# Self-attention of a perceiver layer: queries and values placed in other ways, and the tile's steps in another order

## What is computed

```
x = x + xattn(layernorm(x), ctx, ctx, mask)          # part 1, 257 context rows
x = x + attn(layernorm(x), Wq, bq, ..., Wo, bo)      # part 2, 32 positions
x = x + ffn(layernorm(x), 8 experts, top 2)          # part 3

def attn(x):                                         # B=128, N=32, D=128, H=16, dk=8
    Q, K, V = (proj(Wq, bq), proj(Wk, bk), proj(Wv, bv))     # (x @ W + b), split in heads
    scores = einsum('bhnd,bhmd->bhnm', Q, K) / sqrt(dk)
    scores = scores + power_law_mask(N, 0.25)        # -0.25 log(i-j); -inf above the diagonal
    out = einsum('bhnm,bhmd->bhnd', softmax(scores), V)
    return out @ Wo + bo
```

## Time and profile before

| | us |
|---|---|
| median of 3 runs (lowest, highest) | 981.73 (981.18, 982.58) |
| the profiled execution: its own time | 979.43 |
| its span in the profile | 977.7 |
| PE / DVE / ACT / POOL busy in the span | 828.2 / 829.6 / 661.4 / 448.4 |

### The profile page before, as it was taken

How to read it: one execution, slowest core, us unless ns; L and a number is a source line. 1 busy time by engine, 2 the same in 40 slices (tenths; PEclk the granted TensorE clock), 3 DMA queues, 4 the chain that set the end, 5 groups by cost and what they waited for, 6 DMA issues and landing times. The chain is left out here.

```text
span 977.7 us, 30213 instructions
## 1 busy us (share of the span) xinstructions
PE 828.2 (85%) x9453; PEld 668.0 (68%) x9453; DVE 829.6 (85%) x2343; ACT 661.4 (68%) x2102; POOL 448.4 (46%) x437
## 2 busy tenths in 40 slices
PE   4989889898889988896788888887989889889892
PEld 2666656666666666664678888887888788788782
DVE  4888889888898988986688887874899999999994
ACT  3677777777677777774676666663777677677674
POOL 3222222222222222221454444443677887787785
PEclk9999999999999999999799998999999999999997
DMA  3221111111111111131000000000000000000000
GB/s 85 75 73 49 48 39 49 36 49 48 36 49 41 46 49 38 49 104 61 1 1 0 0 0 0 0 1 1 1 7 11 5 5 11 5 5 11 5 5 17
DMA packets 32695, 27.26 MB, mean 28 GB/s; under 512 B 3548, under 2 KB 32408, under 8 KB 32664
## 3 DMA queue, kind: packets, MB, share of 16 engines
q1 hardware_dynamic: 32664, 26.87, 9.5%
HBM read 24.76 MB, written 2.10 MB: 27 GB/s over the span
## 5 line engine op out<-in xcount | busy, mean ns | idle before, releaser
L545 ACT ACTIVATE E<-SC,neg_max 128x257 f32<-128x257 f32 x512 | 235.9, 474 | 101.7 <-DVE neg_max L605 101.7
L605 DVE TENSOR_REDUCE neg_max<-SC 128x1 f32<-128x257 f32 x512 | 181.9, 418 | 36.4 <-PE SC L402 33.6
L415 PE MATMUL ETP<-ident,E 128*128 128x128 f32 x1024 | 162.8, 287 | 37.7 <-ACT E L545 37.3
L614 DVE TENSOR_TENSOR Et<-ETP,mask_T 128x512 f32<-128x512 f32 x256 | 172.6, 684 | 15.9 <-PE ETP L415 14.8
L415 PEld LDWEIGHTS ETP<-ident,E 128*128 128x128 f32 x1024 | 109.4, 142 | 88.3 <-issue 78.7
L1337 PE MATMUL PO<-W,hid 128*128 128x128 f32 x1024 | 138.1, 278 | 18.8 <-ACT hid L1378 18.8
L1402 ACT ACTIVATE Y<-Z,zb,zs 128x128 f32<-128x128 f32 x256 | 111.0, 485 | 59.9 <-DVE zb L1557 59.9
L1337 PEld LDWEIGHTS PO<-W,hid 128*128 128x128 f32 x1024 | 131.4, 192 | 29.0 <-issue 21.6
L1326 PE MATMUL PH<-xT,W 128*128 128x256 f32 x512 | 135.1, 387 | 0.5 <-ACT xT L1370 0.5
L1378 ACT ACTIVATE hid<-PH,b1c 128x256 f32<-128x256 f32 x256 | 105.5, 463 | 19.4 <-PE PH L1326 17.8
L545 ACT ACTIVATION_READ_ACCUMULATOR E<-SC,neg_max 128x1 f32 x512 | 103.8, 203 | 0.0
(11 more groups left out here) (163 smaller groups left out, 1551.3 us busy)
## 6 DMA issues: line engine op xcount, KB each, us to landing
V<-in_ctx_dram SPq DMA_DIRECT2D x64, 256.0 KB, 2.7
xh<-in_x_dram SPq DMA_DIRECT2D x32, 64.0 KB, 2.2
last_rep<-in_ctx_dram SPq DMA_DIRECT2D x128, 2.0 KB
X<-in_x_dram SPq DMA_DIRECT2D x32, 64.0 KB
out_dram<-Xo SPq DMA_DIRECT2D x64, 32.0 KB, 1.5
W<-in_L_ffn_w_dram SPq DMA_DIRECT2D x1, 1024.0 KB
W<-in_L_ffn_w_dram SPq DMA_DIRECT2D x2, 512.0 KB
b2r<-in_L_ffn_b_dram SPq DMA_DIRECT2D x1, 512.0 KB
```

The costliest lines, as they stand in the source:

```text
L415: i = pe.transpose(ETP[s][:, c:c + P], E[:, j // HB, NQ * (j % HB) + 2 * s + u, k * P:(k + 1) * P], ident[:, :])
L545: i = act.activation(E[:, h, at, :], SC[:, u, 0:S], ACT.Exp, bias=neg_max[:, j % 2, u:u + 1], accum_out=den[:, h, at:at + 1])
L605: dve.tensor_reduce(neg_max[:, j % 2, u:u + 1], SC[:, u, 0:S], AX.X, ALU.max, negate=True).then_inc(max_sb, 1)
L614: dve.tensor_tensor(Et[:, 2 * (j % 2) + s, :, :, :].rearrange("p u k c -> p (u k c)"), ETP[s][:, :], mask_T[:, :, :, :].rearrange("p u k c ...
```

## The change

- **Queries.** `Qt` and `front` are gone. ACT writes `Qbd` straight from `PA`, 4 instructions of 128x256 (one for each q), with `hh_scaled` as per-partition scale and `bq_own` (a new constant, mask times bias, one small DVE instruction in the setup) as per-partition bias.
- **Values.** `xT4`, `repeated` and `Vbd` are gone. PE computes each 32x32 block by itself: weights are a batch of `xT` (128x32), the moving operand is 32 columns of `Wv`, and the output goes to the 32 partitions of its group in one bank `PV`. That is 32 matmuls a tile in place of 8. ACT copies the whole bank, 128x256, in one instruction to `Vt`, which has two buffers, as `xT` now has.
- **Weighing.** In place of a 128x128 matmul with a block diagonal, four of 32 rows x 32 columns, one for each g, on the diagonal tiles of the array: 32 matmuls a tile in place of 8, each still with 128 moving columns.
- **Order.** PE does `project_out` two tiles late (t-2) and right behind `scores(t, 0)`; before, it stood last in the body, for t-1. DVE has `add(t-2)` behind the second `less_maxima`, and `sums(t, 0)` behind both. Two bodies more, of T and T+1, finish the last tiles.
- **No hardware loop** in `attend`: all tiles are in straight line. The clear of `Vbd` in the setup is gone.

```diff
+                dve.tensor_scalar(bq_own[:, :], hh_scaled[:, :, 0], bcol[:, 0:1], None, ALU.mult).then_inc(dve_set2, 1)
-                pool.memset(Vbd[:, :, :], 0.0).then_inc(pool_set2, 1)
 def run(body, eng):
-            body(0, 2, False)
-            body(1, 2, True)
-            with eng.Fori(2, T - 2) as t:
-                body(t, 2, True)
-            body(T - 2, 1, True)
-            body(T - 1, 0, True)
+            for t in range(T - 2):
+                body(t, True, True, t > 0, t > 1)
+            body(T - 2, True, False, True, True)
+            body(T - 1, False, False, True, True)
+            body(T, False, False, True, True, False)
+            body(T + 1, False, False, False, True, False)
 # DVE body (conditions left out)
                     maxima(t, 1)
-                    sums(t, 0)
                     less_maxima(t, 1)
+                    add(t - 2)
+                    sums(t, 0)
                     invert(t, 0)
                     own(t - 1, 0)
                     own(t - 1, 1)
                     norm(t + 2)
                     sums(t, 1)
                     invert(t, 1)
-                    add(t - 1)
 # POOL body
-                    bias(t - 1)
+                    bias(t - 2)
                     power(t + 2)
-                    front(t + 1)
                     normalise(t, 0)
                     normalise(t, 1)
 # ACT
-                    act.activation(Qt[:, :, :].rearrange("p b l -> p (b l)"), PA[:, 0:256], ACT.Identity,
-                                   bias=bcol[:, 0:1]).then_inc(qt_sb, 1)
+                    for q in range(HQ):
+                        i = act.activation(Qbd[:, :, q, :], PA[:, 0:256].rearrange("p (b l) -> p b l", b=TB), ACT.Identity,
+                                           bias=bq_own[:, q:q + 1], scale=hh_scaled[:, q, 0:1])
+                    i.then_inc(q_bd, 1)
-                    for g in range(NQ):
-                        r = slice(32 * g, 32 * g + 32)
-                        i = act.activation(Vbd[r, HB * h:HB * h + HB, 32 * g:32 * g + 32],
-                                           PV[h][r, :, 32 * g:32 * g + 32], ACT.Copy)
+                    act.activation(Vt[:, t % 2, :, :], PV[:, :, :], ACT.Copy).then_inc(v_sb, 1)
 # PE
-                    for j in range(HB):
-                        i = pe.matmul(PV[h][:, j, :], xT4[:, HB * h + j, :, :].rearrange("p g l -> p (g l)"), W["v"][:, :],
-                                      start=True, stop=True)
+                    for b in range(TB):
+                        for g in range(NQ):
+                            i = pe.matmul(PV[32 * g:32 * g + 32, b, :], xT[:, t % 2, b, :], W["v"][:, 32 * g:32 * g + 32],
+                                          start=True, stop=True)
                     for j in range(HB):
-                        i = pe.matmul(PE_[h][:, j, :], Vbd[:, HB * h + j, :], Et[:, h, j, :], start=True, stop=True)
+                        for g in range(NQ):
+                            r = slice(32 * g, 32 * g + 32)
+                            i = pe.matmul(PE_[h][r, j, :], Vt[r, t % 2, HB * h + j, :], Et[r, h, j, :], start=True, stop=True)
```

More of the change, by code:

```diff
@@ L69, in perceiver_layer @@
         bcol = sb("bcol", [P, 3])
+        bq_own = sb("bq_own", [P, HQ])
         out_bias = sb("out_bias", [P, D])
@@ L721, in _ @@
                 turn_tile(T - 1)
-        attend(nc, X, ident, hh_scaled, (W, hh_wide, decay, out_bias, bcol, neg_half2, Kbd, Vbd))
+        attend(nc, X, ident, hh_scaled, (W, hh_wide, decay, out_bias, bcol, bq_own, neg_half2, Kbd))
         mix_experts(nc, X, ident, (G, W1, W2, b1c, b2r, gr, b_rows, iota_f, neg_half3, w3_in), out)
@@ L738, in sem @@
             return s2.enter_context(nc.semaphore(name))
-        W, hh_wide, decay, out_bias, bcol, neg_half, Kbd, Vbd = consts
+        W, hh_wide, decay, out_bias, bcol, bq_own, neg_half, Kbd = consts
         stat = sb("stat2", [P, 2, 6])
@@ L745, in attend @@
         xn = sb("xn2", [P, 2, D])
-        xT = sb("xT2", [P, TB, L])
-        xT4 = sb("xT4", [P, TB, NQ, L])
-        Qt = sb("Qt2", [P, TB, L])
+        xT = sb("xT2", [P, 2, TB, L])
+        Vt = sb("Vt2", [P, 2, TB, L])
         Qbd = sb("Qbd2", [P, TB, HQ, L])
@@ L758, in attend @@
         PA = ps("PA", [P, 512])
-        PV = [ps(f"PV{h}", [P, HB, D]) for h in range(2)]
+        PV = ps("PV", [P, TB, L])
         PS = [ps(f"PS{h}", [P, 512]) for h in range(2)]
@@ L861, in add, with body @@
                     dve.tensor_tensor(tile_of(t), PY[:, :], Xb[:, :], ALU.add).then_inc(x2, 1)
-                def body(t, after, before):
-                    if after > 1:
+                def body(t, one_more, two_more, one_back, two_back, now=True):
+                    if two_more:
                         norm_stats(t + 2)
-                    add_decay(t, 0)
-                    if after > 1:
+                    if now:
+                        add_decay(t, 0)
+                    if two_more:
                         norm_mean(t + 2)
-                    maxima(t, 0)
-                    if after > 1:
+                    if now:
+                        maxima(t, 0)
+                    if two_more:
                         norm_var(t + 2)
-                    add_decay(t, 1)
-                    less_maxima(t, 0)
-                    maxima(t, 1)
-                    sums(t, 0)
-                    less_maxima(t, 1)
-                    invert(t, 0)
-                    if before:
+                    if now:
+                        add_decay(t, 1)
+                        less_maxima(t, 0)
+                        maxima(t, 1)
+                        less_maxima(t, 1)
+                    if two_back:
+                        add(t - 2)
+                    if now:
+                        sums(t, 0)
+                        invert(t, 0)
+                    if one_back:
                         own(t - 1, 0)
                         own(t - 1, 1)
-                    if after > 1:
+                    if two_more:
                         norm(t + 2)
-                    sums(t, 1)
-                    invert(t, 1)
-                    if before:
-                        add(t - 1)
+                    if now:
+                        sums(t, 1)
+                        invert(t, 1)
                 for t in range(2):
@@ L998, in probs, with body @@
                     act.activation(Et[:, h, :, :], PE_[h][:, :, :], ACT.Copy).then_inc(et_sb, 1)
-                def body(t, after, before):
-                    if after > 0:
+                def body(t, one_more, two_more, one_back, two_back, now=True):
+                    if one_more:
                         turned(t + 1)
-                    if before:
+                    if one_back:
                         probs(t - 1, 0)
                         probs(t - 1, 1)
-                    exponentials(t, 0)
-                    if after > 0:
+                    if now:
+                        exponentials(t, 0)
+                    if one_more:
                         projected(t + 1)
[L1009 to L1013, removed]
+                    if now:
+                        exponentials(t, 1)
+                        values(t)
                 turned(0)
                 projected(0)
-                repeated(0)
                 run(body, act)
-                probs(T - 1, 0)
-                probs(T - 1, 1)
             @block.tensor
@@ L1088, in project_out, with body @@
                     i.then_inc(y_ps, 1)
-                def body(t, after, before):
-                    if after > 0:
+                def body(t, one_more, two_more, one_back, two_back, now=True):
+                    if one_more:
                         turn(t + 1)
-                    scores(t, 0)
-                    if before:
+                    if now:
+                        scores(t, 0)
+                    if two_back:
+                        project_out(t - 2)
+                    if one_back:
                         turn_probs(t - 1, 0)
-                    scores(t, 1)
-                    if before:
+                    if now:
+                        scores(t, 1)
+                    if one_back:
                         turn_probs(t - 1, 1)
-                    if after > 0:
+                    if one_more:
                         project(t + 1)
-                    values(t, 0)
-                    if before:
+                    if now:
+                        values(t)
+                    if one_back:
                         weigh(t - 1, 0)
                         weigh(t - 1, 1)
-                    values(t, 1)
-                    if before:
-                        project_out(t - 1)
                 turn(0)
```

73 lines of the change are left out of this document (23 added, 50 removed).

## The result

| | before | after |
|---|---|---|
| median of 4 runs each (lowest, highest), us | 982.15 (981.18, 983.01) | 950.89 (949.44, 952.09) |
| ratio, with its 95% interval | | 0.9681 [0.9665, 0.9698] |
| the profiled execution: its own time, its span | 979.43, 977.7 | 950.97, 949.1 |
| `attend`: first DVE instruction to first score addition | 10.9 | 12.1 |
| first score addition of tile 0 to that of tile 15 | 181.5 | 150.4 |

The kernel became 31 us faster, 28.6 of it in the spans of the two profiled executions. All of it lies between the first additions of tiles 0 and 15: 31.1 less, and 3.0 more at the two ends of `attend`. `attend` itself begins 0.4 earlier. The medians differ by 2.7 more than the spans, because before's profiled execution (979.43) lies 2.7 under its median of 982.15, and that of after (950.97) lies at its own.

A forecast was written before the change was run, and what follows sets the result against it. A loop of waits in `attend`, with a 2.1 us stall behind POOL's product, was taken as the bound. 15 x (10.2 + 0.5) - 2 = 158.5 for 181.5, +1.9 at start and end: -21.1, so 960.6; range 950 to 976.

The forecast's parts named there:

- likeliest case: Main forecast for the whole kernel: 960.6 us, by itself reaching from 955 to 967, chance 0.53.
- rival 4: More gain in `attend`: no stretch at 1.2 GHz, 15 tiles at 10.2 us, 953 in all; chance 0.12.
- The stall: DVE's second `less_maxima` took 2.79 us for 0.68 beside POOL's `Qbd` product; 2.1 a tile should go with it.
- The loop: `attend`, per tile: DVE from second addition to `norm` 5.6, PE from transpose to second scores 4.6; 10.2 us for 11.42.
- the two tied sides: From second addition to transpose, DVE's part and ACT's side (queries, then keys) take 5.6 us each.
- Queries by ACT: Four query copies on ACT at 0.45 us each, 1.8 together, ahead of the keys' 1.88, which the transpose awaits.
- Values and weighing: PE's small tiles: values 0.9 us (ends 0.6 and 1.9), weighing 1.94 a tile, diagonal tiles running side by side.
- Rivals 1 and 2: First of these: PE fed too slowly in values and weighing, 11.2 us a tile, 971; chance 0.17. Second: see rival 2.
- rival 2: Weighing's diagonal tiles run one after another, 3.4 us a half, 14.5 a tile, 1025 in all; chance 0.08.
- Idle time and `own`: PE idle 1.7 us a tile before the transpose; second `own` starts 6.9 after the first addition, just in time.
- Clock: Stretches of PE at 1.2 GHz in `attend` cost 0.5 us a tile, for 0.68; ends nothing and 1.5.
- Start and end: Query copies before first scores +0.9, last tile +1.9, setup -0.9 us: together +1.9; first two tiles 1.0 shorter each.

The follow-up runs named there:

- b_actq: Kernel before with only the queries changed: ACT writes `Qbd` from the projection's bank, POOL's product gone; 945.88 us, ratio 0.9636.
- a_poolq: Changed kernel with queries back on POOL (`Qt` by ACT, product by POOL), order, values and weighing as changed; 965.39 us, ratio 0.9829.
- a_idle: Changed kernel with one more ACT copy of 128x512 a tile, between `Qbd` and `Kbd`, that nobody reads; 968.24 us, ratio 0.9854 to before.
- b_fill: Kernel before with eight extra unused float32 matmuls of 128x128 on PE ahead of the output projection's wait for `own`; 971.11 us, ratio 0.9890.
- a_best: Changed kernel's work in another order on PE and DVE, with projection(t+1) ahead of the output projection and values last; 927.21 us, ratio 0.9444.
- a_old: Changed kernel with the same work in the old order on all engines, project_out(t-1) last on PE, add(t-1) last on DVE; 937.89 us, ratio 0.9557.
- a_mid: Changed kernel with one line moved: project_out(t-2) on PE behind scores(t, 1) instead of ahead; 944.00 us, ratio 0.9612 to before.
- b_valw: Kernel before with only the new values and weighing, and `attend` in straight line; queries from POOL, old order; 982.62 us, ratio 0.9997.

## Why the prediction came out so

**The number.** 950.89 stands 9.7 under the 960.6 forecast, outside the 955 to 967 of the likeliest case and 0.9 above the lower end of the range. The range holds it only because it was widened to rival 4, which had a chance of 0.12. Of the 9.7, 7.4 are between the profiled execution (950.97) and its forecast of 958.3; the other 2.3 were added because before's profiled execution lay that far under its median, and that of after doesn't.

**The stall (right).** 2.1 us a tile left with POOL's product; b_actq shows this with nothing else changed, and PE's long wait for `own` went with it. a_poolq narrows it: in the new order `less_maxima` keeps its 0.69 with the product still on POOL, because it starts ahead of it.

**The loop (right).** 10.2 was worked out, 10.14 measured, with the 5.6 and 4.6 at 5.68 and 4.46, and the two tied sides ending 0.06 apart. The tie is shown by a_idle: 0.5 on ACT's side lengthens the loop by 0.53. The first two tiles are 0.35 and 1.04 shorter than the others, for 1.0 each.

**Queries by ACT (right).** Four in 1.91, the keys 1.79 behind their start: 0.45 each. One instruction by itself takes 0.556 (mean of 56), where L968 with one pointer takes 0.46. By the Trainium skill (ScalarE: Activation LUTs, section "What ACT_TABLE_LOAD costs"), one more pointer operand adds some 93 ns; the trace agrees, with 0.10.

**Values and weighing (right in size).** `values` takes 0.70 from its start to that of the weighing (0.9 taken, bounds 0.6 and 1.9); both halves of the weighing 1.95 (1.94 taken). Rivals 1 and 2 fall by these rows. For rival 2 the Trainium skill (TensorEngine Tiling (Array Packing), section "Gotcha 1: PSUM Pressure") says that different row tiles cannot access one PSUM bank at once; here four diagonal tiles write one bank, each to 32 partitions of its own, and 64 recorded matmuls take 1.95, which is what the output projection's 16 over the whole array take. The measurement decides: they ran side by side.

**Idle time and `own` (right).** PE was to stand 1.7 before the transpose and stands 1.84. `own` starts 6.43 behind the first addition, with no wait.

**Clock (the step that was mis-sized).** "A shorter idle stretch should make it rarer: 0.5 a tile, for 0.68." In the middle of after there is no stretch at 1.2 GHz at all, so the term is 0. That is 7.5 of the 8.1 us by which 158.5 exceeds 150.4, and puts the result on rival 4 (953). b_fill shows the size of the whole effect in before, 11 us. PE's longest regular wait in a tile, and what its clock did:

| | wait of PE, us | stretches at 1.2 GHz in the middle |
|---|---|---|
| a_best, b_actq, b_fill, a_old | about 0, 0.3, 0.3, 0.85 | none |
| a_mid, after | 1.8, 1.84 | none |
| a_idle, a_poolq | 2.37, 2.39 | in every fourth tile |
| before, b_valw | 2.13, up to 2.9 | in seven of the twelve tiles |

The direction of the argument (a shorter wait, fewer such stretches) holds in the two pairs in which one edit changes the wait, before and b_fill, after and a_idle. The step from 2.13 to 1.84 was taken as a partial gain, and it was the whole. The prediction had no row that could tell this; a_idle then shows how little lies between: with half a microsecond more of waiting they are back. The waits don't order the rows fully (before waits less than a_idle and has more of the stretches), so what the chip goes by is not told by them.

**Start and end.** 1.18 for 0.9 at the start, 1.8 for 1.9 at the end. In the setup PE begins part 1 0.9 earlier, as forecast (16.23 for 17.12), but only 0.4 of it is left where `attend` begins; where part 1 loses the rest was not traced.

**What was not asked.** The prediction took the change's order as given, and worked out only the loop that it makes. a_old and a_mid show what that loop contains for nothing: the output projection's 1.9 stands between the scores of the two halves, and DVE's second addition, with all that follows it there, waits behind it. By the forecast's own terms the loop without it is 5.6 + 2.7 = 8.3, below what the other waits allow; a_mid realises 0.41 a tile of this, a_old 0.92; the rest of what a_old moves back, DVE's order with it, was not run apart. Added in one sequence, the queries gave 36 us alone; values, weighing and the straight line nothing alone and 8 behind the queries; the order cost 13 of it. What an edit is worth hangs on the others, as four runs with the same values, weighing and straight line show (b_valw still has the clear of `Vbd` in the setup):

| us | old order | new order |
|---|---|---|
| queries by POOL | 982.62 (b_valw) | 965.39 (a_poolq) |
| queries by ACT | 937.89 (a_old) | 950.89 (after) |

With POOL's product in place the new order gains 17 us: the second `less_maxima` takes 0.69 there for 2.69. With the product gone it costs 13. In the new order the queries are worth 14.5 us, in the old one 44.7. What remains open is how much of the 8 each of values, weighing and the straight line gives; that was not run apart.

## What to carry to other kernels

When an instruction takes four times its usual duration without a wait, look for what runs at the same time on another engine: here it was POOL's product, and taking it away was worth more than the whole change, while starting ahead of it saved a part. A cheaper step pays only on an engine for which the tile waits: the same edit was worth nothing in one setting and 8 us in another. The new order gained 17 us beside the stall and cost 13 without it, so lay out the order anew against the loop that is left, keep long independent work (here the output projection) out of it, and read the granted clock beside PE's wait, which here was worth 6% of the loop by itself.

## What the runs showed of the hardware

- POOL's product held different DVE instructions to a different degree: a `less_maxima` that starts 0.11 behind it took 2.79 for 0.68, one that starts 0.48 ahead of it took 0.69 in a_poolq, and two `own`, which read PSUM, kept their 1.22 beside it there. Two `norm` took 1.29 for 0.59 in a_poolq, 0.09 behind the start of POOL's `En` of 1.04.
- Small tiles were cheaper to issue than was allowed for: `values`, 64 recorded matmuls with 64 weight loads, in 0.76.
- Eight matmuls a tile whose results nobody reads made the kernel before 11 us faster: a tile at full clock kept its 11.42, and the stretches at 1.2 GHz in the middle were gone.
- A copy that holds ScalarE for 0.5 us a tile cost 17 us: 8.0 through the loop, 6.7 through TensorE's clock, 0.5 at the start of `attend`, and 2.3 in part 1, without a known cause.
